# Two-layer graph attention on one Trainium2 core: high and low product operands placed at multiples of sixteen words

## The chip, the core and the metric

One core of a Trainium2 chip runs the whole program. The metric is the device time of one execution in microseconds (us). The engines are TensorE (PE for its products, PEld for loading the stationary operand), VectorE (DVE), ScalarE (ACT), GpSimd (POOL) and SyncE (SP), which issues the DMAs. Each engine works through a program of its own, written out by hand, and waits on semaphores.

## The reference, cut to what matters

The inputs are 1250 nodes with 768 features and 21250 edges sorted by destination. Three graph attentions follow each other, each a softmax over the edges into a node, with normalisations, residual products and gains between them.

```python
# attention 0: 12 heads of 64, then x = layernorm(x + relu(agg + x @ Wres))
# attention 1: 4 heads of 256
xl = x @ W1
e = leaky_relu(alpha_src[src] + alpha_dst[dst], 0.2)
alpha = softmax of e over the edges into dst
h = relu(layer_norm(sum alpha * xl[src] + b1)) + (x @ Wr1 + br1)
# attention 2: 1 head of 768
y = layer_norm(attention(h @ W2) + b2) + (h @ Wr2 + br2)
out = layernorm(x + y)
```

## The kernel before, in words

The 1250 nodes are ten tiles, nine of 128 rows and one of 98. Edge counts are turned into a dense 1250x1250 matrix of logarithms (`LC`), and each attention is then dense. For each head and each destination tile VectorE forms a row tile of 128x1250 scores (`leaky`), adds `LC` and takes the extreme value (`least`), ScalarE applies the exponential, TensorE turns the row tile around in ten 128x128 transposes, the turned tile is copied out of PSUM, and TensorE multiplies it with the features.

The program has five stages: the counting of edges and the projection (0 to 99 us), attention 0 (99 to 444 us), the products with W1 and Wr1 (`gemm1`, L998 to L1014), attention 1 (`use1`, L1053 to L1066), the products with W2 and Wr2 (`gemm2`, L1083 to L1106) and attention 2 (`use2`, L1119 to L1145). From `gemm1` on, every operand of a product is split in two: a high part, which is the value rounded to fp32r by ScalarE, and a low part, which is the rest, found by VectorE or GpSimd. Three products then stand for one: high by high, high by low, low by high.

```python
# L1009: x1T is the stationary operand (128 columns), w1 the moving one (256 columns)
for n, (k, (xs, ws)) in enumerate(steps):
    last = e.matmul(gemm_bank1(p)[0:m, 0:C1], xs[:, i * KT + k, 0:m], ws[b % WBUFS1][:, k, :], ...)
# L1061: et (turned exponentials) stationary, xl moving
for s in range(NT):
    for step, (cols, xs) in enumerate(((et_hi, xl_hi), (et_hi, xl_lo), (et_lo, xl_hi))):
        last = e.matmul(acc1[r % 2][0:w, :], cols[r % 2][0:m, s, 0:w], xs[h % 2][0:m, s, :], ...)
# L1101 and L1140: each stationary tile is used for 512 and for 256 moving columns
        for c, w in halves:
            last = e.matmul(acc2[v % 2][0:m, c:c + w], hs[v % 2][:, k, 0:m], ws[k][:, c:c + w], ...)
```

`gemm1` makes 80 output tiles (8 column blocks b of W1 and Wr1 by 10 node tiles) of 18 products each, 1440 in all; block b uses weight buffer b % 3. Blocks 0, 1 and 2 are worked tile by tile together, blocks 3, 4 and 5 one after the other, blocks 6 and 7 together (`order1`, L441 to L444). `use1` makes 40 row tiles (4 heads by 10) of 30 products, 1200 in all. `gemm2` makes 20 output tiles (`v`, ten with W2 and ten with Wr2) of 8 weight tiles by 3 products, 480 pairs of a 512-column and a 256-column product. `use2` makes ten row tiles of 30 pairs.

SBUF is laid out by hand. After the small tiles (L77 to L93) come six regions (L106 to L114), in this order: `LC`, `rowbuf`, `colbuf`, `R1`, `R2`, `R3`. All tiles of the stages are views into them (`view`, L131), and the fp32r tiles are laid over them again by `overlay` (L116 to L127), which names for each its region and its start in words. A word is four bytes of each partition. The allocator rounds each tile's size up to eight words, and the regions are rounded to eight words too (L101).

Counted in words from the first small tile, the small tiles before take 800 words, and `LC` begins at 800, `rowbuf` at 13304, `colbuf` at 15808, `R1` at 17344, `R2` at 27584 and `R3` at 37848. What matters below is the remainder of a tile's start by sixteen:

- at 8: everything that lies in `R3` (`x1T_hi` and `x1T_lo`, the four `xl` tiles and four `et` tiles of attention 1, `h1T`, one pair of `et2` tiles, five `xl2_lo` tiles, some weights), in `rowbuf`, and whatever begins at 5000 = RING0 * N words of `R1` (weight buffer 2 with both its parts, the low part of weight buffer 1, `wr2` tiles 4 to 6, the other pair of `et2` tiles), and two `xl2_lo` tiles at 2504 words of `R1`
- at 0: weight buffer 0 with both its parts and the high part of weight buffer 1 (`R1`, 0 to 4608), the weights of `gemm2` in `LC` (`w2` 4 to 7, `wr2` 0 to 3) and `colbuf`, `xl2_hi` in `R2`, three `xl2_lo` tiles in `R1`, `ident`

So every stationary operand of a split product begins at 8 by sixteen, and the moving ones begin at 8 or at 0. Steps inside a tile are whole multiples of 128 words.

Attention 0 and all transposes use plain fp32. Their row tiles (`ring`, 1250 words each) begin where the row length puts them.

Of the kernel before, what the change touches and what calls it, by code (L numbers as in the profile page):

```python
# [15 lines left out]
P = 128  # L16
# [11 lines left out]
def gnn_kernel(nc, x, src, dst, W0, attn_l, attn_r, Wres, W1, a_src1, a_dst1, b1, g1, be1, Wr1, br1,  # L28
               W2, a_src2, a_dst2, b2, g2, be2, Wr2, br2, out):
    N, D = x.shape  # L30
# [3 lines left out]
    H1, C1 = a_src1.shape  # L34
    HC = H1 * C1
    NT = (N + P - 1) // P
# [33 lines left out]
    with ExitStack() as ctx:  # L70
        def sbuf(name, free, dt=F32, parts=P):
            return ctx.enter_context(nc.sbuf_tensor(name, [parts] + list(free), dt))
# [5 lines left out]
        loop_only = sbuf("loop_only", [P])  # L78
        w0_diag = loop_only
        att = sbuf("att", [NT, 2 * H0])  # L80
        diag_count = sbuf("diag_count", [NT])
        diag_ln = sbuf("diag_ln", [NT])
        row_max = sbuf("row_max", [RING])
        recip0 = sbuf("recip0", [2, H0])
        den0 = sbuf("den0", [NT, H0])
        stats = sbuf("stats", [2, 6 * H1])
        moments = sbuf("moments", [NT, 2])
        rstd = sbuf("rstd", [NT])
        minus_half = sbuf("minus_half", [1])
        tiny = sbuf("tiny", [1])  # L90
        recip = sbuf("recip", [8])
        zero = recip[:, 0:1]
        shift2 = sbuf("shift2", [2])  # L93
        psum = ctx.enter_context(nc.psum_tensor("psum", [P, 8, BANK], F32))

        regions = ctx.enter_context(ExitStack())
        region_at = {}
        region_words = []

        def region(name, words):  # L100
            words = (words + 7) // 8 * 8  # L101
            region_at[name] = sum(region_words)
            region_words.append(words)
            return regions.enter_context(nc.sbuf_tensor(name, [P, words], F32))

        LC2 = region("LC", NT * N)  # L106
        LC = LC2[:, 0:NT * N].rearrange("p (a b) -> p a b", a=NT)
        row_words = region("rowbuf", 2 * N)
        rows_flat = row_words[:, 0:2 * N]
        rowbuf = rows_flat.rearrange("p (a b) -> p a b", a=2)  # L110
        colbuf = region("colbuf", 3 * BANK)
        R1 = region("R1", RING * N + NT * 2 * H0)
        R2 = region("R2", NT * HC + 2 * NT)
        R3 = region("R3", 2 * NT * D)  # L114

        def overlay(stack, *places):  # L116
            made, at = [], 0
            for name, reg, start, shape in places:
                start += region_at[reg]
                assert start % 8 == 0 and start >= at  # L120
                if start > at:
                    stack.enter_context(nc.sbuf_tensor(f"{name}_before", [P, start - at], F32))
                words = (shape[0] * shape[1] + 7) // 8 * 8
                t = stack.enter_context(nc.sbuf_tensor(name, [P, words], F32R))
                made.append(t[:, 0:shape[0] * shape[1]].rearrange("p (a b) -> p a b", a=shape[0]))
                at = start + words
            return made  # L127
# [3 lines left out]
        def view(region, start, shape, dt=F32, parts=P):  # L131
            n = 1
            for s in shape:
                n *= s
            words = n if dt in (F32, F32R, I32) else n // 2
            ap = region[0:parts, start:start + words]
            if dt != F32:
                ap = ap.bitcast(dt)
            if len(shape) == 2:
                ap = ap.rearrange("p (a b) -> p a b", a=shape[0])  # L140
            if len(shape) == 3:
                ap = ap.rearrange("p (a b c) -> p a b c", a=shape[0], b=shape[1])
            return ap
# [63 lines left out]
        RING0, SETS0 = 4, 3  # L207
# [19 lines left out]

        BLOCKS1, WBUFS1 = 2 * H1, 3
        w1_words = KT * C1
        w1_at = [(0, w1_words), (2 * w1_words, RING0 * N + 2 * w1_words), (RING0 * N, RING0 * N + w1_words)]  # L230
        w1_raw = [view(R1, lo, [KT, C1]) for hi, lo in w1_at]
        br1_at = [3 * w1_words, RING0 * N + 3 * w1_words]
        b1_b = view(rows_flat, 2 * N - HC, [HC])
        xl1 = view(R2, 0, [NT, H1, C1])
        h_buf = view(R2, 0, [NT, HC])
# [5 lines left out]
        rowsT1 = view(rows_flat, 0, [N], F32, H1)  # L241
        assert br1_at[0] + C1 <= RING0 * N and br1_at[1] + C1 <= RING * N and (2 + RES1) * C1 <= colbuf.shape[1]
        RING1 = 4
        junk1 = view(R1, RING * N, [C1], BF16)
        junk_loop = view(R1, RING * N + C1 // 2, [P], BF16)
        ring1 = view(R1, RING1 * N, [RING1, N])
        row_bufs1 = [[rowbuf[:, 0, :], rowbuf[:, 1, :]], [ring[:, 0, :], ring[:, 1, :]]]
        turn1 = turn0
        acc1 = [psum[:, 6 + b, 0:C1] for b in range(2)]
        res1_at = [2 * N + 4 + b * HC for b in range(2)]  # L250
        res1_back = [view(R1, at, [HC]) for at in res1_at]
        vecs1 = view(R3, 0, [2, HC])
        assert res1_at[1] + HC <= RING1 * N


        w2_words = 2 * D
# [1 line left out]
        w2_at = [("R3", 2 * HC), ("R3", 2 * HC + w2_words), ("rowbuf", 0), ("colbuf", 0)]  # L258
        w2_at += [("LC", j * w2_words) for j in range(4)]
        wr2_at = [("LC", (4 + j) * w2_words) for j in range(4)]  # L260
        wr2_at += [("R1", RING1 * N + j * w2_words) for j in range(3)] + [("R3", 2 * NT * C1)]
        W2_EARLY = 4
        xl2_at = [("R1", j * D) for j in range(3)]
        xl2_at += [("R3", 2 * NT * C1 + w2_words + j * D) for j in range(4)] + [("R3", 4 * NT * C1 + 4 * HC)]
# [9 lines left out]
        rowsT2 = view(rows_flat, 0, [2, N], F32, 1)  # L274
        ring2 = view(R3, 0, [RING1, N])
        assert 2 * D <= 2 * N and 5 * D <= RING1 * N + D and RING1 * N <= 2 * NT * C1
        y_bufs = [view(R3, 2 * NT * C1 + b * D, [D]) for b in range(2)] + x1_back
        BASE_TILES = 3
        et2_at = [("R3", 2 * NT * C1 + w2_words + 4 * D + p * NT * P) for p in range(2)]
        et2_at += [("R1", RING1 * N + p * NT * P) for p in range(2)]  # L280
        base_at = RING1 * N + 2 * NT * P
        base_sb = [view(R1, base_at + b * D, [D]) for b in range(BASE_TILES)]
        g2_b = view(R3, 4 * NT * C1 + 2 * HC, [D])
        assert et2_at[1][1] + NT * P <= 4 * NT * C1 + 2 * HC and base_at + BASE_TILES * D <= RING * N
# [5 lines left out]
        with ExitStack() as layer1:  # L290
            w1_places = sorted((at, f"w1_{part}_{b}") for b in range(WBUFS1)
                               for at, part in zip(w1_at[b], ("hi", "lo")))
            w1_tiles = overlay(layer1, *[(name, "R1", at, [KT, C1]) for at, name in w1_places],
                               ("x1T_hi", "R3", 0, [NT * KT, P]), ("x1T_lo", "R3", NT * D, [NT * KT, P]))
# [3 lines left out]
        with ExitStack() as attention1:  # L298
            xl_hi_even, xl_lo_even, xl_hi_odd, xl_lo_odd, et_hi_0, et_lo_0, et_hi_1, et_lo_1 = overlay(
                attention1, *[(f"xl_{name}", "R3", b * NT * C1, [NT, C1]) for b, name in enumerate(  # L300
                    ("hi_even", "lo_even", "hi_odd", "lo_odd"))],
                *[(f"et_{name}", "R3", 4 * NT * C1 + b * NT * P, [NT, P]) for b, name in enumerate(
                    ("hi_0", "lo_0", "hi_1", "lo_1"))])
# [12 lines left out]
        with ExitStack() as products2:  # L316
            made2 = {place[0]: tile for place, tile in zip(places2, overlay(products2, *places2))}
# [1950 lines left out]
```

## Time and profile before

| | us |
|---|---|
| median of three runs (lowest to highest) | 1125.5 (1124.93 to 1126.39) |
| the profiled execution, its own time | 1126.05 |
| its span | 1124.3 |
| busy in the span: PE, DVE, ACT, POOL | 1055.4, 953.4, 642.3, 142.0 |

The profiled execution is told by its span, from the first to the last instruction of the program; its own time holds 1.75 us around the span. A matmul's duration in the trace runs from its issue to its modelled end and overlaps with the next one, so the pace of a stream of products is the distance from start to start, not the duration. The chain of waits gives merged pieces with a count: a piece of 30 products that takes 3.60 us has a pace of 120 ns. In the timeline each line carries its start.

### The profile page before, as it was taken

To read this page: it belongs to the slowest core of one execution; us is meant where nothing else is said; L and a number is where in the kernel's file an instruction comes from. 1 tells how busy PE (TensorE), PEld (TensorE's weight loads), DVE (VectorE), ACT (ScalarE), POOL (GpSimd) and SP (SyncE) were. 2 spreads that over 40 slices of the span, in tenths; PEclk is the share of its full clock that TensorE was granted. 3 is DMA by queue.
4 is the path that set the end of the run, shared out by engine and by line. 5 is a ranking of instruction groups with operands and counts; after the bars stand their busy time and mean duration, and the time that the engine had idled before them with its cause. 6 is when DMAs were issued, how large, how long until landed. Compare 5 with 4: busy or idle time off the path is not lost.

```text
span 1124.3 us, 20566 instructions
## 1 busy us (share of the span) xinstructions
PE 1055.4 (94%) x8048; PEld 909.0 (81%) x8048; DVE 953.4 (85%) x1531; ACT 642.3 (57%) x939; POOL 142.0 (13%) x155
## 2 busy tenths in 40 slices
PE   6986999998989989999999999999999999999996
PEld 4665666666666667999999999999988888888885
DVE  7989999999999999986853999999987873497865
ACT  8658899999999898223111567666612311234331
POOL 1000000000000000000073112020400153311111
PEclk9998999999999999999999999999999999999999
DMA  4061020202020205533237310204041124343211
GB/s 149 1 228 51 3 92 1 93 1 92 2 92 1 98 1 194 172 103 120 80 101 267 129 47 2 84 1 151 20 169 57 43 95 173 131 160 127 76 62 53
DMA packets 40022, 98.99 MB, mean 88 GB/s; under 512 B 4505, under 2 KB 17393, under 8 KB 39925
## 3 DMA queue, kind: packets, MB, share of 16 engines
q1 hardware_dynamic: 39926, 97.66, 25.1%
q8 instruction: 66, 1.08, 0.4%
q14 instruction: 30, 0.25, 0.1%
HBM read 70.74 MB, written 26.90 MB: 87 GB/s over the span
## 4 chain that ended last, share of the span: by engine, by line
PE 65%; DVE 16%; ACT 12%; issue 6%; DVEq 0%; POOL 0%; DMA 0%; SPq 0%; POOLq 0%; ACTq 0%
PE psum L1103 14%; PE psum L1012 14%; PE psum L1064 12%; PE psum L1142 8%; DVE R L1685 7%; ACT R L1281 6%; ACT R L1297 4%; DVE R L1671 4%; PE psum L1027 4%; PE psum L759 3%; PE psum L944 2%; PE psum L1080 1%; DVE LC L1657 1%; PE psum L1133 1%; PE psum L1115 1%
## 5 line engine op out<-in xcount | busy, mean ns | idle before, releaser
L944 PE MATMUL psum<-ident,R 128*128 128x128 f32 (+3 forms) x1200 | 158.5, 281 | 37.5 <-ACT R L1281 37.1
L944 PEld LDWEIGHTS psum<-ident,R 128*128 128x128 f32 (+3 forms) x1200 | 129.1, 143 | 78.0 <-ACT R L1281 65.6
L1685 DVE CUSTOM_DVE_ANT_0 R<-R,LC 128x1250 f32<-128x1250 f32 x120 | 173.8, 1451 | 0.2 <-DVE LC L1657 0.2
L1281 ACT ACTIVATE R<-R,row_max 128x1250 f32<-128x1250 f32 x120 | 161.8, 1348 | 2.0 <-DVE row_max L1685 1.6
L958 PE MATMUL psum<-R 128*64 128x256 f32 (+3 forms) x1200 | 147.5, 384 | 0.6 <-ACT R L1297 0.6
L1297 ACT COPY R<-psum 128x1280 f32<-128x1280 f32 x120 | 144.0, 1200 | 1.5 <-PE psum L944 1.5
L1012 PE MATMUL psum<-w_hi,x1T_hi 128*128 128x256 f32 (+1 forms) x480 | 136.1, 284 | 0.2 <-DVE w_lo L1775 0.2
L1012 PE MATMUL psum<-w_hi,x1T_lo 128*128 128x256 f32 (+1 forms) x480 | 134.8, 281 | 0.0
L1012 PE MATMUL psum<-w_lo,x1T_hi 128*128 128x256 f32 (+1 forms) x480 | 134.4, 282 | 0.0
L1671 DVE SCALAR_TENSOR_TENSOR R<-R 128x1250 f32<-128x1250 f32 x80 | 121.0, 1513 | 0.0
L2160 POOL TENSOR_TENSOR rstd<-rstd,minus_half 128x1 f32<-128x1 f32 (+1 forms) x40 | 33.8, 846 | 664.3 <-DVE rstd L1700 664.3
L958 PEld LDWEIGHTS psum<-R 128*64 128x64 f32 (+1 forms) x1200 | 79.2, 138 | 43.8 <-issue 10.3
L1012 PEld LDWEIGHTS psum<-w_hi,x1T_hi 128*128 128x128 f32 (+1 forms) x480 | 90.1, 188 | 0.8 <-issue 0.4
L1012 PEld LDWEIGHTS psum<-w_hi,x1T_lo 128*128 128x128 f32 (+1 forms) x480 | 89.9, 187 | 0.0
L1012 PEld LDWEIGHTS psum<-w_lo,x1T_hi 128*128 128x128 f32 (+1 forms) x480 | 89.7, 188 | 0.0
L1368 ACT CAST et_hi<-psum 128x1280 fp32r<-128x1280 f32 (+1 forms) x40 | 48.2, 1206 | 56.6 <-PE psum L1027 56.6
L1360 ACT ACTIVATE R<-R,row_max 128x1250 f32<-128x1250 f32 (+1 forms) x40 | 53.7, 1342 | 33.4 <-DVE row_max L1832 33.3
L1966 DVE TENSOR_TENSOR h1T_lo<-psum,h1T_hi 128x1024 fp32r<-128x1024 f32 (+1 forms) x18 | 21.8, 1209 | 55.2 <-ACT h1T_hi L1396 55.2
L1396 ACT CAST h1T_hi<-psum 128x1024 fp32r<-128x1024 f32 (+1 forms) x18 | 18.1, 1006 | 81.8 <-PE psum L1080 81.8
L1907 DVE TENSOR_TENSOR et_lo<-psum,et_hi 128x1280 fp32r<-128x1280 f32 (+1 forms) x40 | 58.2, 1456 | 7.1 <-ACT et_hi L1368 5.7
L1671 DVE SCALAR_TENSOR_TENSOR R<-rowbuf,R 128x1250 f32<-128x1250 f32 (+1 forms) x40 | 60.3, 1512 | 0.6 <-PE psum L944 0.5
L1832 DVE CUSTOM_DVE_ANT_0 R<-R,LC 128x1250 f32<-128x1250 f32 (+1 forms) x40 | 58.7, 1467 | 0.1
(234 smaller groups left out, 2482.6 us busy)
## 6 DMA issues: line engine op xcount, KB each, us to landing
R<-rows_spill SPq DMA_DIRECT2D x20, 625.0 KB, 5.3
rowbuf<-rows_spill SPq DMA_DIRECT2D x14, 625.0 KB, 5.2
lc_spill<-LC SPq DMA_DIRECT2D x9, 625.0 KB
LC<-lc_spill SPq DMA_DIRECT2D x9, 625.0 KB, 5.7
res_spill<-colbuf SPq DMA_DIRECT2D x36, 128.0 KB, 2.9
R<-res_spill SPq DMA_DIRECT2D x9, 512.0 KB, 3.6
R<-in_x_dram SPq DMA_DIRECT2D x1, 3456.0 KB
res_spill<-R SPq DMA_DIRECT2D x9, 384.0 KB
```

The source lines that it names most:

```text
L944: last = e.transpose(turn0[r % 2][0:m, s, 0:n_dst], ring[0:n_dst, r % RING0, s * P:s * P + m], ident[0:n_dst, 0:n_dst])
L958: last = e.matmul(banks[6][k * C0:(k + 1) * C0, 0:w], x_in[0:m, s, (2 * g + k) * C0:(2 * g + k + 1) * C0], exp_bufs0[(2 * n + k) % 4][0:m, ...
L1012: last = e.matmul(gemm_bank1(p)[0:m, 0:C1], xs[:, i * KT + k, 0:m], ws[b % WBUFS1][:, k, :], start=(n == 0), stop=(n == len(steps) - 1))
L1064: last = e.matmul(acc1[r % 2][0:w, :], cols[r % 2][0:m, s, 0:w], xs[h % 2][0:m, s, :], start=(s == 0 and step == 0), stop=(s == NT - 1 and ...
L1103: last = e.matmul(acc2[v % 2][0:m, c:c + w], hs[v % 2][:, k, 0:m], ws[k][:, c:c + w], start=(k == 0 and step == 0), stop=(k == KH - 1 and ...
L1142: last = e.matmul(acc2[r % 2][0:n_dst, c:c + w], cols[r % 2][0:m, s, 0:n_dst], xs[s][0:m, c:c + w], start=(s == 0 and step == 0), stop=(s ...
L1281: e.activation(ring[0:m, r % RING0, :], ring[0:m, r % RING0, :], ACT.Exp, bias=row_max[0:m, r % RING:r % RING + 1], scale=-1.0, accum_out= ...
L1297: e.copy(exp_bufs0[(2 * n + j // 2) % 4][:, :, (j % 2) * P:(j % 2) * P + rows[i]], turn0[r % 2][:, :, 0:rows[i]]).then_inc(S.kept0, 1)
L1671: e.scalar_tensor_tensor(out=ring[0:m, r % RING0, :], in0=row_slope[0:m, :], scalar=att_part0[0:m, i, H0 + h:H0 + h + 1], in1=row[0:m, :], ...
L1685: e.tensor_tensor_reduce(slot, slot, LC[0:m, i, :], -1.0, MIN_CEILING, ALU.add, ALU.min, row_max[0:m, r % RING:r % RING + 1]).then_inc(S.l ...
L1832: e.tensor_tensor_reduce(slot1(r)[0:m, :], slot1(r)[0:m, :], LC[0:m, i, :], -1.0, MIN_CEILING, ALU.add, ALU.min, row_max[0:m, r % RING:r % ...
L1907: e.tensor_tensor(et_lo[r % 2][:, :, 0:w], turn1[r % 2][:, :, 0:w], et_hi[r % 2][:, :, 0:w].bitcast(F32), ALU.subtract).then_inc(S.et_lo, 1)
```

## The change

Regions are rounded up to sixteen words instead of eight, so `LC` takes 12512 words (12504), `rowbuf` 2512 (2504) and `R2` 10272 (10264). The starts inside `R1` that were 5000 words become 5008 (`upper`), and `res1_at` begins at 2512 words instead of 2504. The assert of `overlay` asks for multiples of sixteen. To make room, small tiles share a tensor: `diag_count`, `diag_ln`, `rstd` and `moments` lie in `per_tile` (50 words), and `recip`, `minus_half`, `tiny` and `shift2` in `small` (12 words). The small tiles then take 768 words instead of 800, and the regions begin at 768, 13280, 15792, 17328, 27568 and 37840, each a multiple of sixteen. The sum of all words falls from 53208 to 53200. No instruction is added, removed or moved, and no size of an operand changes.

```diff
@@ -78,27 +78,29 @@
-        diag_count = sbuf("diag_count", [NT])
-        diag_ln = sbuf("diag_ln", [NT])
+        per_tile = sbuf("per_tile", [5, NT])
+        diag_count, diag_ln, rstd = (per_tile[:, k, :] for k in range(3))
+        moments = per_tile[:, 3:5, :].rearrange("p a b -> p (a b)").rearrange("p (a b) -> p a b", b=2)
...
-        moments = sbuf("moments", [NT, 2])
-        rstd = sbuf("rstd", [NT])
-        minus_half = sbuf("minus_half", [1])
-        tiny = sbuf("tiny", [1])
-        recip = sbuf("recip", [8])
+        small = sbuf("small", [12])
+        recip = small[:, 0:8]
+        minus_half, tiny, shift2 = small[:, 8:9], small[:, 9:10], small[:, 10:12]
         zero = recip[:, 0:1]
-        shift2 = sbuf("shift2", [2])
...
+        LINE = 16
+
+        def whole_lines(words):
+            return (words + LINE - 1) // LINE * LINE
 
         def region(name, words):
-            words = (words + 7) // 8 * 8
+            words = whole_lines(words)
@@ -117,7 +119,7 @@
-                assert start % 8 == 0 and start >= at
+                assert start % LINE == 0 and start >= at
@@ -227,9 +229,10 @@
         w1_words = KT * C1
-        w1_at = [(0, w1_words), (2 * w1_words, RING0 * N + 2 * w1_words), (RING0 * N, RING0 * N + w1_words)]
+        upper = whole_lines(RING0 * N)
+        w1_at = [(0, w1_words), (2 * w1_words, upper + 2 * w1_words), (upper, upper + w1_words)]
-        br1_at = [3 * w1_words, RING0 * N + 3 * w1_words]
+        br1_at = [3 * w1_words, upper + 3 * w1_words]
@@ -241,13 +244,14 @@
-        res1_at = [2 * N + 4 + b * HC for b in range(2)]
+        res1_at = [whole_lines(2 * N) + b * HC for b in range(2)]
@@ -258,7 +262,7 @@
-        wr2_at += [("R1", RING1 * N + j * w2_words) for j in range(3)] + [("R3", 2 * NT * C1)]
+        wr2_at += [("R1", upper + j * w2_words) for j in range(3)] + [("R3", 2 * NT * C1)]
@@ -277,8 +281,8 @@
-        et2_at += [("R1", RING1 * N + p * NT * P) for p in range(2)]
-        base_at = RING1 * N + 2 * NT * P
+        et2_at += [("R1", upper + p * NT * P) for p in range(2)]
+        base_at = upper + 2 * NT * P
```

## Rows read from the trace of the kernel before

**Rows 1.** The page: busy times, and the granted clock in 40 slices.
```profile
PE 1055.4 (94%) x8048; PEld 909.0 (81%) x8048; DVE 953.4 (85%) x1531; ACT 642.3 (57%) x939; POOL 142.0 (13%) x155
...
PEclk9998999999999999999999999999999999999999
```

**Rows 2.** Windows by stage: length, PE, PEld, DVE, ACT, POOL busy, clock, DMA.
```profile
99.00:444.00 345.00, 309.92 (x2533) 224.77 (x2533) 344.14 (x371) 315.69 (x432) 0.56 (x1) 0.98 0.15 49
444.00:628.00 184.00, 181.41 (x1535) 180.80 (x1534) 131.40 (x352) 44.27 (x84) 36.48 (x51) 0.99 0.44 149
628.00:814.00 186.00, 185.04 (x1587) 184.52 (x1586) 177.71 (x218) 127.52 (x193) 36.79 (x39) 1.00 0.17 56
814.00:1000.00 186.00, 184.90 (x1122) 162.83 (x1121) 127.21 (x170) 45.77 (x57) 47.17 (x29) 1.00 0.31 107
1000.00:1115.00 115.00, 114.56 (x688) 100.26 (x686) 83.81 (x153) 37.19 (x45) 16.23 (x18) 1.00 0.28 100
```

**Rows 3.** Waits of PE from 444 us to the end: total, times, longest.
```profile
PE psum L995 <- DVE R L1739: 2.4, 1, 2.4
PE psum L1115 <- ACT R L1419: 1.1, 1, 1.1
```

**Rows 4.** The chain in order of time: start, length, instruction, count.
```profile
505.57 71.76 PE psum L1012 x612
...
722.20 3.60 PE psum L1064 x30
...
837.63 8.35 PE psum L1103 x48
...
1058.96 10.54 PE psum L1142 x60
1070.60 10.48 PE psum L1142 x60
```

**Rows 5.** Groups of VectorE instructions, 99 to 444 us: busy, mean ns.
```profile
L1671 DVE SCALAR_TENSOR_TENSOR R<-R 128x1250 f32<-128x1250 f32 x78 | 118.0, 1513 | 0.0
L1671 DVE SCALAR_TENSOR_TENSOR R<-rowbuf,R 128x1250 f32<-128x1250 f32 (+1 forms) x38 | 57.4, 1512 | 0.5 <-PE psum L944 0.5
```

**Rows 6.** Timeline of `gemm1`: two starts 42 products apart in blocks 3, 4, 5.
```profile
525.00 0.28 PE L1012 MATMUL psum<-w_hi,x1T_hi 128*128 128x256 f32 x1
...
529.98 0.28 PE L1012 MATMUL psum<-w_hi,x1T_hi 128*128 128x256 f32 x1
...
544.92 0.28 PE L1012 MATMUL psum<-w_hi,x1T_hi 128*128 128x256 f32 x1
...
549.87 0.28 PE L1012 MATMUL psum<-w_hi,x1T_hi 128*128 128x256 f32 x1
...
570.03 0.28 PE L1012 MATMUL psum<-w_hi,x1T_hi 128*128 128x256 f32 x1
...
574.79 0.28 PE L1012 MATMUL psum<-w_hi,x1T_hi 128*128 128x256 f32 x1
```

**Rows 7.** Timeline of `gemm2`, v = 14: starts of weight tiles 1, 4, 5, 7.
```profile
943.29 0.51 PE L1103 MATMUL psum<-wr_hi,h1T_hi 128*128 128x512 f32 x2
...
946.41 0.51 PE L1103 MATMUL psum<-wr_hi,h1T_hi 128*128 128x512 f32 x2
...
947.45 0.52 PE L1103 MATMUL psum<-wr_hi,h1T_hi 128*128 128x512 f32 x2
...
949.57 0.51 PE L1103 MATMUL psum<-wr_hi,h1T_hi 128*128 128x512 f32 x2
```

**Rows 8.** Loads of the stationary operand by shape, whole span: busy, mean ns.
```profile
L1012 PEld LDWEIGHTS psum<-w_hi,x1T_hi 128*128 128x128 f32 x432 | 82.3, 190 | 0.8 <-issue 0.4 <-DVE x1T_lo L1770 0.3
L1064 PEld LDWEIGHTS psum<-xl_lo_odd,et_hi 128*128 128x128 f32 x162 | 31.0, 191 | 0.0
L1080 PEld LDWEIGHTS psum<-ident,R 128*128 128x128 f32 x136 | 15.5, 140 | 0.8
L995 PEld LDWEIGHTS psum<-ident,R 128*128 128x128 f32 x54 | 6.0, 140 | 2.9 <-DVE R L1739 2.5 <-issue 0.3
```

**Rows 9.** Tile `rstd`: GpSimd's power and VectorE's sum, min/median/max ns.
```profile
L1700 DVE TENSOR_SCALAR rstd<-moments x40: 152/154/156, 437.3 to 1119.7; 128x1 f32<-128x1 f32 x36, 98x1 f32<-98x1 f32 x4
L2160 POOL TENSOR_TENSOR rstd<-rstd,minus_half x40: 543/550/2062, 437.5 to 1120.0; 128x1 f32<-128x1 f32 x36, 98x1 f32<-98x1 f32 x4
```

More of the change, by code:

```diff
@@ L243, in gnn_kernel @@
         RING1 = 4
+        assert RING1 == RING0
         junk1 = view(R1, RING * N, [C1], BF16)
```

## The prediction, made before the changed kernel ran

> **What bounds the kernel now.** I read the page first, then the windows by stage, the waits of TensorE, the chain in order of time, and last the timeline inside the product stages. The page has TensorE busy for 1055.4 of 1124.3 us at nearly full clock [rows 1]. The windows split this. In attention 0 VectorE works 344.1 of 345 us, so this stage is VectorE's. In the four stages behind it TensorE works 666 of 671 us and VectorE less: 131, 178, 127 and 84 us [rows 2]. From 444 us on TensorE's longest waits are 2.4 and 1.1 us [rows 3], so what it gains per product reaches the end one for one, until VectorE becomes the bound. The clock is at its upper level (2.4 GHz) in these stages [rows 2].
>
> The chain gives the pace, start to start: `gemm1` 71.76 us / 612 = 117.3 ns for 256 columns, `use1` 3.60 / 30 = 120.0 ns, `gemm2` 8.35 / 24 = 348 ns for a pair of 512 and 256 columns, `use2` 10.48 or 10.54 / 30 = 349 or 351 ns [rows 4]. 256 columns at 2.4 GHz are 106.7 ns and a pair 320 ns, so a single product costs 11 to 13 ns over its columns and a pair 28 to 31. The loads themselves take 190 ns, overlap with the product before, and keep up [rows 8]. Something stretches the pace, and the change can only bear on that.
>
> Does a start matter at all? `gemm1` answers inside one stage. Block 3 (weight buffer 0, start 0 by sixteen) has 4.98 / 42 = 118.6 ns, block 4 (buffer 1, high part at 0, low part at 8) 4.95 / 42 = 117.9, block 5 (buffer 2, both at 8) 4.76 / 42 = 113.3 [rows 6]. Shapes, stationary tiles and work are the same. The address matters, but not as the change has it: the tiles at a multiple of sixteen are the slow ones, where the stationary operand lies at 8. In `gemm2` it is the other way: weight tiles 1 to 3 (`LC`, at 0) take 3.12 us / 9 = 346.7 ns a pair, tiles 5 and 6 (`R1`, at 8) 2.12 / 6 = 353.3 [rows 7]. And `use1`, with both operands at 8, has the 120.0 of [rows 4]. No row shows a split product whose stationary operand begins at 0.
>
> **The change, part by part.** No instruction, size or order changes; only starts do.
>
> *Attention 0 and before.* The first use of `rowbuf` (at 8 before, at 0 after) and of the rings takes VectorE 1512 and 1513 ns [rows 5]: the start makes no difference there, and VectorE bounds the stage. Cost 0. Bounds: 78 + 38 instructions at one ns either way, 0.1 us.
>
> *Small tiles shared.* The readers are one-column instructions of 152 ns (VectorE) and 550 ns (GpSimd) [rows 9]; their count stays and no wait is added. They lie beside TensorE's work. Cost 0; if the cover were gone, one ns on each of the 40 pairs would be 0.04 us each.
>
> *`gemm1`.* 540 products read buffer 0, 540 buffer 1, 360 buffer 2. After the change moving and stationary operands all agree by sixteen, as only buffer 2's do now. I take the row of the same stage that has this agreement, 113.3 ns: (118.6 - 113.3) x 540 = 2.9 us and (117.9 - 113.3) x 540 = 2.5 us, together -5.4. Bounds: all 1440 at 106.7 from about 117.9 is -16.1; all at `use1`'s 120.0 is +0.8, +1.1 and +2.4, together +4.3.
>
> *`use1`.* Operands agree already and stay so, at 120.0. I take 0. Bounds: (120.0 - 106.7) x 1200 = -16, of which VectorE lets through 186 - 177.7 = 8.3 [rows 2]; above, no row of this shape is slower than 120.0, so at most one ns each, +1.2.
>
> *`gemm2`.* The 240 pairs that read `LC` differ from the stationary operand by 8 now and agree afterwards; the row of this stage with agreement is 353.3 against 346.7: +6.6 ns x 240 = +1.6 us. The other pairs mostly agree now: 0. Bounds: (348 - 320) x 480 = -13.4; all at 353.3, (353.3 - 348) x 480 = +2.5.
>
> *`use2`.* Even and odd row tiles read different stationary places and differ by 2 ns a pair [rows 4]. `xl2_hi` comes to agree, two thirds of the low tiles agree in part already, and the two stages above disagree on the sign. I take 0. Bounds: (350 - 320) x 300 = -9, and 353.3 for all, +1.0.
>
> *The transposes.* `h_buf` begins at 0 and `acc0` at 8, and the loads take 140 ns from both [rows 8]: 0.
>
> *DMAs.* Same count and bytes, no queue passed, behind TensorE's work in these stages: 0. Were they late, TensorE's waits of [rows 3] would grow.
>
> Sum: -5.4 + 1.6 = -3.8 us. The profiled execution's own time is 1126.05 us (span 1124.3 and 1.75 around it), 0.55 above the median of the runs, so the sum gives 1122.25 for it and 1121.7 for a median. All bounds together: -16.1 - 8.3 - 13.4 - 9 = -46.8 (1078.7) and +4.3 + 1.2 + 2.5 + 1.0 = +9.0 (1134.5).
>
> The trace has 113 to 120 ns for 256 columns whatever the start. The Trainium skill (TensorE: Matmul & The Clock Gate, "Back-to-back issue gap") gives N / 2.4 + 2.5 ns, 109.2 here, and (same page, "Step-by-step: what each phase is for") says that loading the next weights does not steal read bandwidth from the running matmul. By that, nothing of the stretch would come from two streams meeting; the rows disagree, since the pace moves with the address of the moving tile alone [rows 6].
>
> **The rivals.** *The stretch goes altogether, or mostly.* If a stationary operand at 8 is what stretches the pace, all four stages gain. Against it: loads of transposes do not care [rows 8]; for it: no split product has been seen without it, and the stretch is there in all of them. The bound is 1078.7; with a quarter of it kept, the gain is 35 us: about 1090.
>
> *The start by sixteen is nothing.* The paces of [rows 6, 7] contradict one another by sixteen, so they may come from something else (which part of the memory, which stage), and then every pace stays. It comes to the same if the first small tile does not itself begin at a multiple of sixteen words, which no row shows: the change would then do what it says only between tiles. 1125.5. The Trainium skill (SBUF — State Buffer, "Specifications (TRN2)") has lines of 16 bytes, four words; by that every tile begins on a line already and the time stays at 1125.5. Rows 6 show an effect of starts that this does not explain.
>
> *Slower: the distance by 32 words decides.* This one explains more rows than my own sum. By 32, the stationary tiles in `R3` lie at 24 now, buffer 0 and `LC` at 0, buffer 2 and `wr2` 4 to 6 at 8. Distance 16 gives 113.3 (buffer 2), distance 0 gives 120.0 (`use1`), distance 24 gives 118.6 (buffer 0); for pairs 24 gives 346.7 and 16 gives 353.3. After the change `R3` and `R1` lie at 16, `upper` and `LC` at 0. Buffer 2 keeps its distance of 16, buffer 0 and the high part of buffer 1 go to 0: (120.0 - 118.6) x 540 + (120.0 - 117.9) x 360 = +1.5 us. `LC` goes to 16: +1.6. Together +3.1 us, 1128.6. It decides from the point where the 900 products of `gemm1` are above 119 ns rather than below 116. Against it: 32 is read from few rows, and the place inside sixteen may count beside it.
>
> **How the numbers follow.** About 0.2% (2.3 us) is what a measurement of this kernel can tell from no change. My sum, faster by a few us: 0.32, and the forecast is its 1121.7. The stretch goes: 0.12, 1090. Nothing: 0.23, 1125.5. Distance: 0.33, 1128.6. The last is as likely as the first; I keep the first as forecast since anything that an operand at a whole line may save comes on top of it and of no other case. Faster 0.44, same 0.23, slower 0.33. Cases of both signs hold the most: the likeliest one's own range is 1113 to 1123. The range of all takes in the distance case with its bound, up to 1132, and down to 1100, which leaves out most of the large gain and the last of the large loss.
>
> **What would show it.** Steps right: the 42 products of a buffer 0 block take 4.76 us and not 4.98; `use1` pieces stay at 3.60 us; `gemm2` pairs of `LC` move up to 353; attention 0 is 345 us as before; TensorE's waits stay under 3 us. Wrong: `use1` falls below 3.50 us for 30 (the large gain, then VectorE would appear among the waits of attention 1), or blocks 3 and 5 still differ by 5 ns (distance, or nothing), or block 3 rises to 120 (distance). An attention 0 of another length would mean that VectorE's operands count, which I excluded.

## The result, and the profile after

The changed kernel took 1128.99 us (median of 12 runs, 1127.31 to 1129.34), the kernel before 1125.99 us (median of 12 on the same chip, 1124.40 to 1127.01). The ratio is 1.0023, with a 95% interval of 1.0016 to 1.0031: slower by 3 us, a little over what can be told from no change. The forecast was 1121.7 and had the sign wrong. The third rival, the distance by 32 words, had said 1128.6.

The profiled execution has a span of 1127.3 us. The windows by stage of the changed kernel (columns as in [rows 2]):

```profile
99.00:444.00 345.00, 309.05 (x2535) 224.17 (x2536) 344.10 (x372) 315.50 (x433) 0.56 (x1) 0.98 0.15 49
444.00:628.00 184.00, 180.70 (x1516) 179.88 (x1516) 129.18 (x347) 43.53 (x83) 36.49 (x51) 0.99 0.43 148
628.00:814.00 186.00, 185.01 (x1587) 184.50 (x1586) 178.08 (x221) 127.80 (x193) 35.54 (x38) 1.00 0.17 57
```

Attention 0 is VectorE's as before, 344.10 us busy of 345. In the window of `gemm1` TensorE got through 1516 matmuls in 180.70 us instead of 1535 in 181.41: fewer per microsecond, and idle for 0.7 us more. Now each stage by its products: attention 0 up to the first product of `gemm1`, `gemm1` and `gemm2` from their first to their last product, attentions 1 and 2 from the last product before them on. Attention 0 lasts 344.3 us in both traces and attention 1 187.6 in both. `gemm1` grew from 182.3 to 184.4 us, `gemm2` from 184.3 to 186.1, and attention 2 went from 116.1 to 115.6. With attention 0 beginning 0.4 us earlier in the changed kernel, that is the whole difference of 3.0 us.

The waits of TensorE from 444 us on, changed kernel (total, times, longest), answer to [rows 3]:

```profile
PE psum L999 <- DVE R L1743: 2.4, 1, 2.4
PE psum L1031 <- ACT R L1364: 0.7, 1, 0.7
PE psum L1016 <- DVE x1T_lo L1774: 0.6, 1, 0.6
```

One of them is new: 0.6 us for `x1T_lo` (the low part of the stationary operand) at 452 us, before the fourth output tile of `gemm1`. The kernel before has no such wait, and its wait of 1.1 us at the start of attention 2 [rows 3] is 0.5 us here, which accounts for the 0.5 that attention 2 is shorter by. Nearly all else that `gemm1` and `gemm2` lost is pace. The chain in order of time of the changed kernel (start, length, instruction, count), against [rows 4]; its lines are four higher:

```profile
506.36 72.20 PE psum L1016 x612
579.64 43.33 PE psum L1016 x360
...
728.68 3.60 PE psum L1068 x30
...
830.29 8.45 PE psum L1107 x48
...
1027.22 10.48 PE psum L1146 x60
1038.79 10.56 PE psum L1146 x60
```

The same piece of the kernel before that [rows 4] does not have:

```profile
578.40 42.80 PE psum L1012 x360
```

612 products of `gemm1` went from 71.76 to 72.20 us, the last 360 (blocks 6 and 7) from 42.80 to 43.33, an output tile of `gemm2` from 8.35 to 8.45 us, while 30 products of attention 1 kept their 3.60 us. Aligned or not, the pace of attention 1 is the same to the last digit.

The timeline of blocks 3, 4 and 5 in the changed kernel, two starts 42 products apart in each, against [rows 6]:

```profile
525.73 0.28 PE L1016 MATMUL psum<-w_hi,x1T_hi 128*128 128x256 f32 x1
...
530.72 0.28 PE L1016 MATMUL psum<-w_hi,x1T_hi 128*128 128x256 f32 x1
...
545.04 0.28 PE L1016 MATMUL psum<-w_hi,x1T_hi 128*128 128x256 f32 x1
...
550.12 0.28 PE L1016 MATMUL psum<-w_hi,x1T_hi 128*128 128x256 f32 x1
...
570.93 0.28 PE L1016 MATMUL psum<-w_hi,x1T_hi 128*128 128x256 f32 x1
...
575.69 0.28 PE L1016 MATMUL psum<-w_hi,x1T_hi 128*128 128x256 f32 x1
```

Block 3 runs at 4.99 / 42 = 118.8 ns (118.6 before), block 4 at 5.08 / 42 = 121.0 (117.9), block 5 at 4.76 / 42 = 113.3 as before. All three have both operands at multiples of sixteen words now, and they still differ by up to 8 ns. Agreement by sixteen is not what made buffer 2 fast. Blocks 6 and 7, measured in the same way over a whole output tile, went from 118.5 and 119.4 ns to 120.1 and 121.0. And the pairs of `gemm2` that read `LC` (weight tiles 1 and 4 of v = 14, nine pairs apart), against [rows 7]:

```profile
946.16 0.52 PE L1107 MATMUL psum<-wr_hi,h1T_hi 128*128 128x512 f32 x2
...
949.34 0.52 PE L1107 MATMUL psum<-wr_hi,h1T_hi 128*128 128x512 f32 x2
```

3.18 / 9 = 353.3 ns a pair, where it was 346.7: exactly the pace that [rows 7] have at a distance of 16 words.

The kernel before has a row on `gemm2` that the prediction did not look at. Weight tile 1 of `W2` lies in `R3` like the stationary operand, so it agrees with it by sixteen, at a distance of 0 words:

```profile
851.90 0.51 PE L1103 MATMUL psum<-w_hi,h1T_hi 128*128 128x512 f32 x2
...
852.94 0.51 PE L1103 MATMUL psum<-w_hi,h1T_hi 128*128 128x512 f32 x2
```

That is 1.04 / 3 = 346.7 ns a pair, the pace of the tiles that do not agree. The same tile takes 353.3 ns in the changed kernel (854.08 to 855.14 us), although its own distance is still 0. So a tile's pace can also follow from its neighbours.

### The profile page after: what moved, and what is told of

Read it like the earlier page. It is cut to its first block, busy times and chain, and to the rows that moved or that the text cites. A ratio compares the mean times of both kernels' runs of the same rounds, so it can differ in the third digit from the quotient of the medians.

```text
span 1127.3 us, 20566 instructions
## 1 busy us (share of the span) xinstructions
PE 1057.5 (94%) x8048; PEld 909.3 (81%) x8048; DVE 952.1 (84%) x1531; ACT 641.9 (57%) x939; POOL 142.9 (13%) x155
## 4 chain that ended last, share of the span: by engine, by line
PE 63%; DVE 19%; ACT 9%; issue 7%; DMA 1%; DVEq 0%; POOL 0%; SPq 0%; POOLq 0%; ACTq 0%
PE psum L1107 14%; PE psum L1016 14%; PE psum L1068 12%; PE psum L1146 8%; DVE R L1689 8%; DVE R L1675 6%; ACT R L1285 5%; PE psum L1031 4%; ACT R L1301 3%; PE psum L763 3%; PE psum L948 1%; PE psum L1084 1%; DVE LC L1661 1%; PE psum L1137 1%; PE psum L1119 1%
## 5 line engine op out<-in xcount | busy, mean ns | idle before, releaser
L2164 POOL TENSOR_TENSOR per_tile<-per_tile,small 128x1 f32<-128x1 f32 (+1 forms) x40 | 33.8, 845 | 665.9 <-DVE per_tile L1704 665.9
```

## The experiments

The theory after this reading: only the distance between the start of the moving and of the stationary operand counts, taken by 32 words (distance = stationary start minus moving start). Rivals: the place of a tile by sixteen counts for itself; or the loss has another source, such as a transfer or a wait in the first tiles.

### Distance kept, place changed: e1 and e2

e1 is the kernel before with all six regions 24 words lower; the small tiles are shared as in the change, and eight words of padding follow. `R3` then begins at a multiple of 32.

```diff
+        per_tile = sbuf("per_tile", [5, NT])      # and small, as in the change
...
+        pad_words = sbuf("pad_words", [8])
         psum = ctx.enter_context(nc.psum_tensor("psum", [P, 8, BANK], F32))
```

> The kernel before with all six regions moved down by 24 words (small tiles packed, eight words of padding): every distance between tiles is that of before, but the stationary tiles in R3 now begin at a multiple of sixteen (and of 32) words and weight buffer 0 begins at 8. Theory A (only the distance between moving and stationary start, by 32 words, counts): as the kernel before, 1126.0 us within 1 us, block 5 of gemm1 at 113.3 ns and pairs of LC at 346.7 ns. Theory B (the place of a tile by sixteen counts for itself): different from before by over 2 us, in the direction of after where stationary tiles at a whole line are what made it slower, so about 1129.

1125.99 us, beside 1126.41 for the kernel before; the ratio, 1.0007 (0.9998 to 1.0017), cannot be told from 1. e2 is the mirror of it, the changed kernel with the same padding, so that all its tiles lie at 8 by sixteen:

```diff
+        pad_words = sbuf("pad_words", [8])
...
-                assert start % LINE == 0 and start >= at
+                assert start % 8 == 0 and start >= at
```

> The changed kernel with all six regions moved up by 8 words: every distance is that of after, but no tile begins at a multiple of sixteen any more, all begin at 8. Theory A (distances): as after, 1129.0 us within 1 us, pairs of LC at 352.7 ns. Theory B (place by sixteen): back towards the kernel before, 1126 us or below.

1128.47 us; ratio 1.0023 (1.0014 to 1.0032), that of the changed kernel. The chain of e1, then of e2:

```profile
504.80 71.76 PE psum L1011 x612
577.62 42.81 PE psum L1011 x360
...
827.64 8.36 PE psum L1102 x48
```

```profile
505.45 72.28 PE psum L1017 x612
578.79 43.33 PE psum L1017 x360
...
829.38 8.45 PE psum L1108 x48
```

e1 has the lengths of before with its stationary tiles at multiples of 16 words, e2 those of after with none of its tiles there. In these pieces the place by itself is worth nothing in either direction, and in the whole time neither the place nor the sharing of the small tiles shows. The theory stands against its first rival. One thing stays open: the output tiles up to the start of block 3 take 74.9 us in e1 and 74.2 in the kernel before, at the same distances. Whether these 0.7 us are chance or place, no run tells.

### The change undone by parts: e5 and e6

e5 is the changed kernel with the lower weight buffers of `gemm1` 8 words up, which gives back the old distances in this stage alone.

```diff
-        w1_at = [(0, w1_words), (2 * w1_words, upper + 2 * w1_words), (upper, upper + w1_words)]
+        low = 8
+        w1_at = [(low, low + w1_words), (low + 2 * w1_words, upper + 2 * w1_words), (upper, upper + w1_words)]
```

> The changed kernel with the lower weight buffers of gemm1 8 words further up, so that every weight of gemm1 has the distance of the kernel before again (24 for buffer 0 and the high part of buffer 1, 16 for the rest), while all other starts stay those of after. Distance theory: block 4 back from 121.1 to 117.8 ns, blocks 6 and 7 from 120.1 and 121.0 to 118.5 and 119.4, gemm1 182.3 us long instead of 184.4 and the whole 1129.0 - 2.1 = 1126.9. If the start of the loss was another one (first tiles of gemm1 waiting for the splits, a transfer), gemm1 stays at 184 us.

1127.81 us, ratio 1.0013 (1.0004 to 1.0022). e6 is the changed kernel with the `gemm2` weights in `LC` 24 words up:

```diff
-        w2_at += [("LC", j * w2_words) for j in range(4)]
-        wr2_at = [("LC", (4 + j) * w2_words) for j in range(4)]
+        w2_at += [("LC", 24 + j * w2_words) for j in range(4)]
+        wr2_at = [("LC", 24 + (4 + j) * w2_words) for j in range(4)]
```

> The changed kernel with the gemm2 weights in LC 24 words further up, at a distance of 24 from the stationary tiles as before. Distance theory: the 240 pairs go from 352.7 back to 346.7 ns or so, gemm2 from 186.1 to about 184.3 us, the whole 1129.0 - 1.8 = 1127.2. If gemm2's loss lay elsewhere: no change, 1129.

1126.28 us, ratio 1.0006 (0.9997 to 1.0015). The chain of e5, then of e6:

```profile
504.19 71.72 PE psum L1017 x612
576.98 42.80 PE psum L1017 x360
...
827.13 8.45 PE psum L1108 x48
```

```profile
504.78 72.20 PE psum L1016 x612
578.05 43.33 PE psum L1016 x360
...
828.64 8.36 PE psum L1107 x48
```

Each returns its own stage to the old lengths and leaves the other as it was. (The whole times alone would not show it: the interval of e5 overlaps with that of the changed kernel.) In the traces `gemm1` lasts 182.2 us in e5, and `gemm2` 184.5 in e6. So the loss has two parts that lie where the theory puts them: about 1.3 us in `gemm1` (e6 and e2, with the changed distances, have 183.6 there) and 1.7 in `gemm2`. The profiled execution of the changed kernel has 184.4 us in `gemm1`; of the 0.8 us left, 0.6 are the wait for `x1T_lo` shown above, which neither e2 nor e6 has at the same distances. So this part does not belong to the distances. The cleanest figure is the time from the first product of block 3 to the last of block 7: it is 108.0 us in all six traces whose distances in `gemm1` are the old ones (before, e1, e4, e5, e7, e8) and 109.0 in all three with the new ones (after, e2, e6). The whole times of e5 and e6 are each 0.9 us from what was expected, e5 above and e6 below.

### Other distances: e3, e4, e7, e8

If distance 16 makes buffer 2 fast, all of `gemm1` could have it. e3 is the kernel before with the lower buffers 8 words up:

```diff
-        w1_at = [(0, w1_words), (2 * w1_words, RING0 * N + 2 * w1_words), (RING0 * N, RING0 * N + w1_words)]
+        low, high = 8, RING0 * N + 0
+        w1_at = [(low, low + w1_words), (low + 2 * w1_words, high + 2 * w1_words), (high, high + w1_words)]
```

> The kernel before with the lower weight buffers of gemm1 moved by 8 words inside R1 (starts 8, 1544, 3080 instead of 0, 1536, 3072), so that all weights of gemm1 stand at a distance of 16 words (by 32) from the stationary tiles, as only buffer 2 does in the kernel before. Theory A: blocks 3, 4, 6 and 7 fall from 118.6, 117.9, 118.5 and 119.4 ns to 113.3; with 90% of 1080 products gaining 5 to 6 ns the time is 1126.0 - 5.5 = 1120.5 us. Theory B' (buffer 2 is fast for where it lies, not for its distance): 1126.0 and blocks 3 and 5 still 5 ns apart.

1124.86 us, ratio 0.9988 (0.9979 to 0.9997): faster, but by a quarter of what was expected. The timeline of e3 in blocks 3 and 5, 42 products apart:

```profile
524.96 0.28 PE L1013 MATMUL psum<-w_hi,x1T_hi 128*128 128x256 f32 x1
...
529.72 0.28 PE L1013 MATMUL psum<-w_hi,x1T_hi 128*128 128x256 f32 x1
...
564.83 0.28 PE L1013 MATMUL psum<-w_hi,x1T_hi 128*128 128x256 f32 x1
...
569.77 0.28 PE L1013 MATMUL psum<-w_hi,x1T_hi 128*128 128x256 f32 x1
```

Block 3 has fallen from 118.6 to 113.3 ns as forecast. But block 5, not one of whose addresses was touched, has risen from 113.3 to 4.94 / 42 = 117.6. In the trace block 3 holds 113.3 until its last output tile, that of the 98 rows, and all that follow stay at 117.6 to 117.9 up to a stall late in block 5. At a distance of 16 the stream of products has two steady paces, and in blocks 3 to 7 it keeps the one that it fell into. In blocks 0 and 2 of e3, where other work stands between the output tiles, it changes between 113.4 and 117.8 ns from tile to tile. What chooses the pace was not settled.

e4 gives attention 1 the distance of 16, which has 0 in both kernels. 16 words are inserted ahead of the `et` tiles in `R3`, in the room that the shared small tiles free:

```diff
+        ET_OFF = 16
+        R3 = region("R3", 2 * NT * D + ET_OFF)
...
-                *[(f"et_{name}", "R3", 4 * NT * C1 + b * NT * P, [NT, P]) for b, name in enumerate(
+                *[(f"et_{name}", "R3", 4 * NT * C1 + ET_OFF + b * NT * P, [NT, P]) for b, name in enumerate(
```

> The kernel before with the small tiles packed and the et tiles of attention 1 moved up by 16 words inside R3, so that moving xl and stationary et stand at a distance of 16 words by 32 instead of 0 (R3 grows by 16, the regions start 32 words lower). Theory A: a piece of 30 products falls from 3.60 to about 3.40 us (113.3 ns each); 1200 x 6.7 = 8 us less for TensorE, and VectorE lets through up to 8.3, so 1118 to 1120 us. Theory B' (the pace of attention 1 has another reason than distance, such as ScalarE and VectorE writing et beside it): 1126.0 and 3.60 us.

1121.51 us, ratio 0.9963 (0.9949 to 0.9977). Chain of e4:

```profile
672.90 3.54 PE psum L1063 x30
...
718.26 3.43 PE psum L1063 x30
```

Most of the 40 row tiles take 3.43 us (114.3 ns), some 3.54 to 3.56 (118 ns), against 3.60. That is short of the 1118 to 1120 us expected, which took the fast pace for all of them. The four row tiles of 98 rows are all among the slow ones, two of them with a slow neighbour right behind, but so is the one ahead of the second of them: a narrow tile cannot be the only thing that changes the pace. Attention 1 lasts 183.0 us instead of 187.6; VectorE is busy for 181 of 186 us in its window, but TensorE still waits for it less than 1 us. e7 and e8 are e4 with `ET_OFF` 8 and 24.

> As e4, with the et tiles of attention 1 at a distance of 8 words (by 32) from the xl tiles instead of 16. Nothing was seen yet at 8 with 256 columns; at a pair of 512 and 256 the distance of 8 had 351 to 353 ns. If distance decides: one steady pace, and not 120.0; I expect about 118.5 as at 24, so attention 1 is 186 us (1200 x 1.5 = 1.8 us less) and the whole 1124.5. If any shift of et away from 0 breaks what slows it: 183.0 us as e4, whole 1121.5.

> As e4, with the et tiles at a distance of 24 words. The same distance has 118.6 ns in block 3 of gemm1: 3.56 us for 30 products, attention 1 near 186 us and the whole 1124.5. If it is as fast as e4 instead (183.0 us, 1121.5), the distance of 16 is nothing special and only 0 is slow.

1124.57 us (ratio 0.9983, 0.9974 to 0.9992) and 1124.20 us (0.9982, 0.9972 to 0.9992). Their chains, e7 and e8:

```profile
721.43 3.55 PE psum L1063 x30
```

```profile
721.64 3.53 PE psum L1063 x30
```

118.3 and 117.7 ns in most of the 40 row tiles (26 of 3.55 us and 27 of 3.53), and both whole times are those expected if distance decides. So in one stage, with the same work beside it, distance 0 gives 120.0 ns, 8 gives 118.3, 24 gives 117.7, and 16 gives 114.3 or 117.8. The distance is not all of it: 24 gives 118.6 ns in `gemm1` [rows 6].

### Starts between the lines, and the period: e9, e10, e12

e9 and e10 are the kernel before with each weight buffer of `gemm1` at a distance of its own (the diff changes the offsets in `w1_at` and lets `overlay` begin a tile inside its tensor).

```diff
-        w1_at = [(0, w1_words), (2 * w1_words, RING0 * N + 2 * w1_words), (RING0 * N, RING0 * N + w1_words)]
+        w1_at = [(16, 1552), (3108, 8132), (5004, 6572)]     # e9; e10: [(20, 1588), (3132, 8124), (5002, 6570)]
```

> A look at the pace only: the kernel before with the three weight buffers of gemm1 each at another distance from the stationary tiles: buffer 0 (block 3) at 8, buffer 1 (block 4) at 20, buffer 2 (block 5) at 12 words. If the distance by 32 words sets the pace, attention 1's 118.6 ns or so at a distance of 8 comes back in block 3, and blocks 4 and 5 have steady paces of their own between 107 and 121 ns; if a place on a multiple of eight words mattered more, blocks 4 and 5 (starts at odd multiples of four words) would be clearly slower than 121.

> The same with distances 4 (block 3), 28 (block 4) and 14 (block 5, starts at 2 words past a multiple of four). Distance theory: paces between 107 and 121 ns, with 14 near the two paces that 16 showed (113.3 or 117.8). A start inside a group of four words costs a clear step more if lines of four words count.

One execution of each, 1127.88 and 1127.37 us against 1126.26. Paces over 42 products in blocks 3, 4 and 5: e9 118.3 (distance 8), 117.6 (20), 120.0 (12); e10 117.9 (4), 118.6 (28), 119.8 (14). Block 3 of e9 is right on what attention 1 shows for 8. No pace here is above what starts at multiples of eight words have shown (120.0 and, for two distances in turn, 121.0), neither for starts at an odd multiple of four words nor for those two words past a multiple of four. That 14 would lie near the paces of 16 was wrong. In e10 block 7 (buffer 1 at 28, its tiles alternating with those of block 6 at 4) ran at 113.3, though the same buffer had 118.6 in block 4: the order of the tiles counts there too.

e12 puts the lower buffers of e3 32 words higher (`low = 40`), which is the same distance by 32 and another by 64.

> As e3, but the lower weight buffers of gemm1 begin 40 words up instead of 8: by 32 words the distance is 16 as in e3, by 64 words it is 48 and not 16. If distances repeat after 32 words: the same paces as e3, block 3 at 113.3 ns and blocks 4 to 7 at 113.3 or 117.8, gemm1 near 181.0 us. If the period is longer than 32 words: block 3 at another pace, between 117 and 121 ns.

One execution, 1126.29 us, beside one of 1126.74 for the kernel before. Timeline in block 3:

```profile
526.81 0.28 PE L1013 MATMUL psum<-w_hi,x1T_hi 128*128 128x256 f32 x1
...
531.76 0.28 PE L1013 MATMUL psum<-w_hi,x1T_hi 128*128 128x256 f32 x1
```

4.95 / 42 = 117.9 ns, and about so (117 to 118 ns) in nearly all output tiles of blocks 3 to 7: the slower pace of distance 16, starts following in the pattern of e3's later blocks (117, 119, 117, 118, 118 ns and on). The expectation for a period of 32 words was 113.3 ns in block 3 and 181.0 us for `gemm1`; the trace has 117.9 and 182.4, which is what was written down for a longer period. It also fits a period of 32 with the stream caught in the slower of its two paces, so e12 does not settle it. The changed kernel has another hint: its buffer 0 stands at a distance of 0 by 32 words but of 32 by 64, and block 3 runs at 118.8 ns, where attention 1, at 0 by both, has 120.0. A period of 64 words would allow for that; so would a difference between the stages. No run tells which.

### What beats both: e11

```diff
+        ET_OFF = 16                                    # as e4
+        low, high = 8, RING0 * N + 0                   # as e3
...
-        wr2_at += [("R1", RING1 * N + j * w2_words) for j in range(3)] + ...
+        wr2_at += [("R1", RING1 * N + 24 + j * w2_words) for j in range(3)] + ...
-        et2_at += [("R1", RING1 * N + p * NT * P) for p in range(2)]
+        et2_at += [("R1", RING1 * N + 16 + p * NT * P) for p in range(2)]
```

> A version meant to beat both: the kernel before with small tiles packed, et of attention 1 at distance 16 (as e4), the lower weight buffers of gemm1 at distance 16 (as e3), wr2 tiles 4 to 6 moved by 24 words in R1 (distance 16 to 24) and the second pair of et2 tiles by 16 words (distance 8 to 24 from xl2_hi). Distance theory, from the pieces: gemm1 -1.3, attention 1 -4.5, gemm2 90 pairs x 6.6 ns = -0.6, attention 2 150 pairs x 1.8 ns = -0.3: 1126.2 - 6.7 = 1119.5 us. If the gains are not additive (the pattern of one stage carried into the next): 1121 or more.

1117.77 us, ratio to the kernel before 0.9919 (0.9905 to 0.9932): 8.5 us faster by the medians (9.1 by the ratio), and 11 faster than the change. The expectation was 1119.5. Chain of e11:

```profile
505.01 71.38 PE psum L1012 x612
577.46 41.03 PE psum L1012 x360
...
717.02 3.43 PE psum L1064 x30
...
1005.16 10.48 PE psum L1142 x60
1016.74 10.49 PE psum L1142 x60
```

`gemm1` took 179.1 us: here blocks 6 and 7 fell into the fast pace (41.03 / 360 = 114.0 ns) and 4 and 5 into the slow one, a luckier draw than e3's, and most of what it beat its expectation by. Attention 1 is that of e4, and in attention 2 the odd row tiles have come down from 10.54 to 10.48 us with their new distance. `gemm2` gained nothing in sum (184.4 us).

## Why the prediction was wrong

**What bounds the kernel: right.** TensorE's pace from 444 us on went into the time one for one; attention 0 kept its 344.3 us, and e1 shows no cost of sharing the small tiles.

**That agreement by sixteen makes the pace: wrong, and this step carried the sign.** The term of -5.4 us for `gemm1` took buffer 2's 113.3 ns as the price of agreement. In the changed kernel all three blocks agree and have 118.8, 121.0 and 113.3 ns. Buffer 2 can be fast because of its distance of 16 words, which the change left alone (e3 brings block 3 down to 113.3 ns by giving it that distance). Instead of falling by 5.4 us the stage grew by 1.3 us for distance, plus 0.8 in the first tiles of the profiled execution, 0.6 of them a wait. The text had a row against this step: `use1` agreed by sixteen and had 120.0 ns, and I let the row of the same stage outweigh it.

**`gemm2`: right in size.** +1.6 us was forecast from 353.3 against 346.7 ns; 353.3 was measured, and 1.8 us for the stage. The reason given was wrong. Agreement by sixteen does not make a pair slow: weight tile 1 of `W2` agreed in the kernel before and took 346.7 ns. What the slow tiles share is a distance of 16 words. e6 takes it from the tiles in `LC` and they are back at 346.7; e11 takes it from the tiles in `R1`, and they fall from 353.3 to 346.7. That the size came out right for the wrong reason is luck.

**`use1`, `use2`, transposes, DMAs: right as zero.** 3.60 us, 10.48 and 10.56 us (10.54 before). The count of waits was not quite as forecast: the 0.6 us for `x1T_lo` is new, still under the 3 us that the prediction allowed.

**The rival that came true.** Its sum of +3.1 us hit the +3.0. By stage it had +1.5 and +1.6 us, and the distances cost 1.3 and 1.7 to 1.8. That the rest of the profiled difference (+0.8, -0.5 and -0.4 us, see the stages above) cancels out is luck, and inside `gemm1` the parts are not as it said. It had buffer 0 going to 120.0 ns, and block 3 stayed at 118.8; instead block 4, whose high weights now stand at 0 and low ones at 16, went to 121.0, above any pace that a single distance had shown, and blocks 6 and 7 rose by 1.6 ns each. Two distances in turn are not the mean of two paces. I kept it at the chance of my own forecast although it explained more rows, on the argument that whole lines might save something on top. e2 against the changed kernel shows that they save nothing.

**The large gain.** The stretch over 106.7 ns did not go with alignment. The Trainium skill (TensorE: Matmul & The Clock Gate, "Step-by-step: what each phase is for") says that loading the next weights does not take bandwidth from the running matmul. Here the pace of products whose loads overlap them lies between 113.3 and 121.0 ns, and in most of the blocks and stages in which the distance between the two starts was changed it moved (not in block 3 of the changed kernel, 118.6 to 118.8). That is hard to square with two streams that run free of each other, and the measurement decides. It is argued and not shown that these two streams are the ones that meet: each run that changed this distance also changed the one to the tiles that other engines use. The formula of the same page that the prediction cites is another matter. The Trainium skill (TensorE: Matmul & The Clock Gate, "Back-to-back issue gap") gives it for an isolated matmul and not for a stream, so paces above its 109.2 ns do not contradict it.

The Trainium skill (SBUF — State Buffer, "Specifications (TRN2)") has lines of 16 bytes and a penalty for each cross to a new line. From that one would estimate that a start inside a line costs something, since a row then crosses one line more. e10's block 5 does not show it, with 119.8 ns beside 120.0 for e9's, whose tiles start on a multiple of four words; but the two stand at different distances (14 and 12), so this is no clean test.

## What to carry to other kernels

Where split fp32r products follow one another with a load for each, the place of an operand is not worth aligning further for its own sake; what moves the pace is the distance between the starts of moving and stationary operand, here from 113.3 to 120.0 ns at 256 columns (distances taken by 32 words; the period is not settled), and beside it what ran before. Measure it per stage from start to start, and try a few offsets of 8 words for one operand. At 256 columns a distance of 0 was the slowest multiple of eight in attention 1; for the pairs of `gemm2` it was not. When one row of the trace supports a mechanism and another with the same property contradicts it, look for the property in which they differ before pricing anything.

## What was not expected of the hardware

- The distance between two tiles counts and their common place does not: moving all tiles together by 24 or 8 words leaves each merged piece of the chain within 0.1 us (71.76 and 71.76, 43.33 and 43.33 us).
- At a distance of 16 words the same stream has two steady paces, 113.3 and 117.8 ns, and can stay in one for hundreds of products. In e3 it changed at an output tile with a narrower stationary operand (98 rows); that this was the cause is not shown. So a change in one block can slow another block whose addresses it does not touch (e3, block 5).
- For a pair of 512 and 256 columns the order is another: 346.7 ns at a distance of 24, 353.3 at 16, and at 0 either of the two, with the tiles around it.
